# Transposing the second norm's rows by DMA instead of on TensorE, in a fused WKV mixer and mixture-of-experts kernel

## What is computed

```
x = x + wkv(w, u, layernorm(x), ctx)                     # 2048 rows of 512
y = layernorm(x)
probs = softmax(y @ gate_w.T);  top 2 of 8 experts per row
moe = sum over the 2 chosen e of prob_e * (silu(y @ gate_e.T) * (y @ up_e.T)) @ down_e.T     # width 256
shared = sigmoid(y @ g.T) * (silu(y @ sg.T) * (y @ su.T)) @ sd.T                             # width 1024
x = x + moe + shared
```

## Time and profile before

| | |
|---|---|
| median of 3 runs | 564.96 us (562.85 to 565.99) |
| profiled execution | 566.06 us, its span 564.3 us |
| PE busy (TensorE) | 486.2 us, 86% |
| DVE busy (VectorE) | 421.3 us, 75% |
| POOL busy (GpSimd) | 345.4 us, 61% |
| ACT busy (ScalarE) | 275.9 us, 49% |
| DMA | q0 (GpSimd's) 21.3%, q1 (SyncE's) 18.5% of the 16 engines' span, the latter for 37.59 MB |
| chain that ended last | PE 52%, POOL 17%, issue 10%, DVE 9%, DMA 7%, ACT 3% |

### The profile page before, as it was taken

One profiled execution on the slowest core, in us unless ns is written; L12 is line 12 of the kernel. 1 busy time (PEld: TensorE's weight loads), 2 busy tenths in 40 slices (PEclk: granted clock), 3 DMA queues, 4 the chain that ended last, 5 costly groups with the idle time before them and its releaser, 6 DMA issues.

```text
span 564.3 us, 10142 instructions
## 1 busy us (share of the span) xinstructions
PE 486.2 (86%) x2671; PEld 258.5 (46%) x2671; DVE 421.3 (75%) x954; ACT 275.9 (49%) x534; POOL 345.4 (61%) x422
## 2 busy tenths in 40 slices
PE   1116789899999999999999979999999999999970
PEld 1113345345455555454555435445545555555530
DVE  5678987899989899999898867566656656666650
ACT  4848837575573864765837333433333333333310
POOL 5767956857948669588486364334375565555332
PEclk9999989999999999999999999999999999999995
DMA  7970105105213223151101320315576776677453
GB/s 283 415 271 19 38 19 187 57 21 188 76 46 143 77 82 143 38 188 62 52 20 39 105 88 15 113 45 102 101 122 117 141 119 116 110 131 123 69 73 38
DMA packets 25929, 59.14 MB, mean 105 GB/s; under 512 B 6314, under 2 KB 6314, under 8 KB 24338
## 3 DMA queue, kind: packets, MB, share of 16 engines
q0 software_dynamic: 9824, 20.90, 21.3%
q1 hardware_dynamic: 16050, 37.59, 18.5%
HBM read 37.83 MB, written 20.65 MB: 104 GB/s over the span
## 4 chain that ended last, share of the span: by engine, by line
PE 52%; POOL 17%; issue 10%; DVE 9%; DMA 7%; ACT 3%; SPq 1%; POOLq 0%; DVEq 0%; ACTq 0%
PE GU L884 28%; PE DN L899 14%; DMA out<-wall,idsa 5%; POOL wall L445 4%; PE XT L829 3%; PE HT L829 3%; POOL yb L429 2%; POOL nrm L411 2%; POOL nrm L413 2%; DVE wall L1071 2%; POOL wall L424 2%; POOL wall L421 2%; DVE wall L1078 1%; PE YT L829 1%; SPq L366 1%
## 5 line engine op out<-in xcount | busy, mean ns | idle before, releaser
L884 PE MATMUL GU<-wall,xt 128*128 128x512 f16 x768 | 187.0, 384 | 2.1 <-DVE wall L1173 2.0
L899 PE MATMUL DN<-wall,hx 128*128 128x512 f16 (+1 forms) x618 | 150.8, 380 | 7.2 <-DVE hx L1200 4.5
L884 PEld LDWEIGHTS GU<-wall,xt 128*128 128x128 f16 x768 | 74.8, 99 | 70.4 <-issue 3.7
L584 POOL DMA_INDIRECT out<-wall,idsa x39 | 62.0, 1590 | 73.1 <-SPq L370 35.1
L659 ACT ACTIVATE hx<-HT 128x256 f16<-128x256 f32 x103 | 39.0, 379 | 127.4 <-PE HT L829 110.6
L899 PEld LDWEIGHTS DN<-wall,hx 128*128 128x128 f16 x618 | 60.4, 98 | 81.9 <-issue 6.0
L1200 DVE TENSOR_TENSOR hx<-HT,hx 128x256 f16<-128x256 f32 x103 | 43.1, 418 | 64.3 <-ACT hx L659 59.7
L654 ACT ACTIVATE th<-GU,scl 128x256 f32<-128x256 f32 x103 | 48.5, 471 | 80.0 <-PE GU L884 76.1
L884 PE MATMUL GU<-wall,kb 128*128 x240 | 61.4, 379 | 0.2 <-DVE kb L1374 0.2
L884 PE MATMUL GU<-wall,xnb 128*128 x228 | 58.5, 379 | 0.6 <-DVE xnb L1374 0.6
L574 POOL DMA_INDIRECT xb<-xn_rows,idsi x39 | 40.2, 1030 | 30.5 <-DMA out<-xb 16.3
(11 more groups left out here) (163 smaller groups left out, 747.3 us busy)
## 6 DMA issues: line engine op xcount, KB each, us to landing
wall<-wgu SPq DMA_DIRECT2D x12, 1024.0 KB, 9.7
wall<-wd SPq DMA_DIRECT2D x12, 512.0 KB, 10.3
out<-xb SPq DMA_DIRECT2D x20, 256.0 KB
xb<-x SPq DMA_DIRECT2D x16, 256.0 KB, 2.7
cb<-ctx_t SPq DMA_DIRECT2D x16, 256.0 KB
xn_rows<-xnb SPq DMA_DIRECT2D x16, 256.0 KB
xb<-xn_rows,idsi POOLq DMA_INDIRECT x39
out<-wall,idsa POOLq DMA_INDIRECT x39
```

The source lines that it names most:

```text
L584: pool.indirect_dma_start(out, bass.IndirectOffsetOnAxis(ap=idsa[:, j:j + 1], axis=0), ye[j % RESULTS], None, compute_op=ALU.add).then_inc ...
L884: ins = nc.tensor.matmul(GU[par][:], lhs(xp, c), gate_up(base, wp, c), start=m == 0, stop=m == 3 * HC - 1)
L899: ins = nc.tensor.matmul(DN[:], hx[par][:, hp * IE + c * P:hp * IE + (c + 1) * P], down(base, wp, c), start=start and m == 0, stop=stop an ...
```

## The change

The second norm's rows are split into halves where they are rows, and the pair is transposed by a DMA on SyncE's queue.

- **Mix.** `norm` puts the factor XS = 1024 into the scale. ScalarE writes xnb in float32 and then, in a second instruction over the same row, the high half as float16 into a new buffer xr. VectorE makes the low half as xnb minus the high half, from SBUF. SyncE then issues `turn_xn`, one DMA transpose of 128 x 1024 float16 (256 KB) from xr into xt, eight blocks of 128 x 128. The four transposes of XT, `xn_t_` and `act_hi` are gone, and the bank XT too. `store_xn` stores the pair xr (as many bytes as before) and waits for the low half.
- **Order in the mix.** On VectorE `act_lo` stands before the last reciprocal and before `hidden(n + 2)` instead of after it. On SyncE the store of the sum goes ahead of the transpose, the store of xn and the load of x behind it. The router and the shared units wait for the transpose (`x_turned`).
- **End of the mix.** SyncE's queue after the last turn is: `turn_xn(15)`, then the load of expert 7, then the stores.
- **Routed phase.** The gather brings rows that are already split. `gathered_t`, `gathered_hi` and `gathered_lo` are gone; one DMA transpose per slot (`turn_gathered`) writes one of now four buffers xe. The first four are issued before the last `store_sum`. The transpose of slot j+3 stands in SyncE's queue at the head of step j, that is behind the permission of add j-1 and ahead of that of add j. It waits for its gather and for the slot four before to be used up. A gather into a buffer waits for the transpose that read it.
- Small tables move into the context buffer cb to make room, and less_r shrinks to four columns that are broadcast.

The core of the diff (declarations, semaphore lists and small moves of tables left out):

```diff
+        xr = sb("xr", [P, 2 * H], F16)
...
-        xe = [kb[:, :].bitcast(F16), xnb[:, :].bitcast(F16)]
+        xe = [kb[:, :].bitcast(F16), xnb[:, :].bitcast(F16), xt[:, 2 * H:4 * H], yb[:, :].bitcast(F16)]
+        XE = len(xe)
...
+            def turn_xn(t):
+                sp.wait_ge(x_lo, t + 1)
+                wait_from(sp, x_turned, t * 16)
+                wait_from(sp, gu, (t - NX + 1) * SU)
+                wait_from(sp, logits, t - NX + 1)
+                sp.dma_start(span(xt, (t % NX) * (2 * H), 2 * H).rearrange("p (c t) -> p c t", t=P), xr[:],
+                             transpose=True).then_inc(x_turned, 16)
+            def turn_gathered(j):
+                r = j % GATHERS
+                sp.wait_ge(gather[r], 16 * (j // GATHERS + 1))
+                if j >= XE:
+                    sp.wait_ge(gu, N_EXP + j - XE + 1)
+                    sp.wait_ge(g_turned[j % XE], 16 * (j // XE))
+                sp.dma_start(xe[j % XE].rearrange("p (c t) -> p c t", t=P), xg[r][:, 0:H].bitcast(F16),
+                             transpose=True).then_inc(g_turned[j % XE], 16)
             def store_xn(t):
-                sp.wait_ge(xn_rdy, t + 1)
-                sp.dma_start(rows(xn_dram, t)[:, 0:H], xnb[:]).then_inc(xn_st, 16)
+                sp.wait_ge(x_lo, t + 1)
+                wait_from(sp, xn_st, t * 16)
+                sp.dma_start(rows(xn_dram, t)[:, 0:H], xr[:, :].bitcast(F32)).then_inc(xn_st, 16)
...
-                if i == 1:
-                    load_expert(1)
...
-                if i > 0:
+                if i > 0 and j is None:
+                    turn_xn(i - 1)
                     store_xn(i - 1)
+                    load_expert(1)
                 if j is not None and j > 0:
                     store_sum(j - 1)
+                if j is not None:
+                    turn_xn(i - 1)
+                    store_xn(i - 1)
...
             sp.wait_ge(y_rdy, B)
+            turn_xn(B - 1)
             load_expert(E - 1)
...
+            for j in range(XE):
+                turn_gathered(j)
             store_sum(B - 1)
             sp.wait_ge(waits_rdy, WAIT_STEPS)
             for j in range(1, NSLOT):
+                if j + XE - 1 < NSLOT:
+                    turn_gathered(j + XE - 1)
...
             def second_norm(t):
                 act.wait_ge(norm2, (t + 1) * NORM_STEPS)
-                wait_from(act, xn_t, t)
-                wait_from(act, xn_st, 16 * t)
+                wait_from(act, x_lo, t)
                 nc.scalar.activation(xnb[:], xrow(t), ACT.Identity, bias=nrm[:, 1, 3:4],
                                      scale=nrm[:, 1, 2:3]).then_inc(xn_rdy, 1)
+                wait_from(act, xn_st, 16 * t)
+                wait_from(act, x_turned, 16 * t)
+                nc.scalar.activation(xr[:, 0:H], xrow(t), ACT.Identity, bias=nrm[:, 1, 3:4],
+                                     scale=nrm[:, 1, 2:3]).then_inc(x_hi, 1)
...
-                pe.wait_ge(g_lo, j + 1)
+                pe.wait_ge(g_turned[j % XE], 16 * (j // XE + 1))
...
             def act_lo(t):
+                dve.wait_ge(xn_rdy, t + 1)
                 dve.wait_ge(x_hi, t + 1)
-                STT(xt_row(t, 1), XT[:], XS, xt_row(t, 0), ALU.mult, ALU.subtract).then_inc(x_lo, 1)
+                TT(xr[:, H:2 * H], xnb[:], xr[:, 0:H], ALU.subtract).then_inc(x_lo, 1)
...
                 hidden_lo(n + 1, 1)
+                act_lo(i - 1)
                 reciprocals(i, 3, 1)
                 hidden(n + 2, 0, SHARED)
-                act_lo(i - 1)
```

More of the change, by code:

```diff
@@ L175, in build @@
         r_cmp, r_eid, r_row, r_one, r_of = taken(NSLOT * E), taken(NSLOT), taken(E), taken(E), taken(2)
+        eidi, idsi, idsa, wsl, pad_of = (taken(NSLOT) for _ in range(5))
+        eidi, idsi, idsa, before_i = (a.bitcast(I32) for a in (eidi, idsi, idsa, taken(RESULTS * NSLOT)))
         ids_back, ids_float = by_time[0:NSLOT, 0:P * LW].bitcast(I32), yb[0:NSLOT, 0:P]
@@ L410, in norm @@
                 wait_from(pool, used, t)
-                nc.gpsimd.tensor_scalar(nrm[:, k, 0:1], mv[:, k, 1:2], EPS, None, ALU.add).then_inc(steps, 1)
+                nc.gpsimd.tensor_scalar(nrm[:, k, 0:1], mv[:, k, 1:2], EPS, XS ** -2 if k else 1.0, ALU.add,
+                                        ALU.mult).then_inc(steps, 1)
                 pool.wait_ge(steps, t * NORM_STEPS + 1)
@@ L506, in _ @@
             second_product(1)
-            norm(0, 1, agg2, norm2, xn_rdy)
+            norm(0, 1, agg2, norm2, x_hi)
             scales(1, SHARED)
@@ L527, in turn @@
                     shared_d_lo(0)
-                norm(i - 1, 1, agg2, norm2, xn_rdy)
+                norm(i - 1, 1, agg2, norm2, x_hi)
                 if i == LAG:
@@ L549, in _ @@
             expert_lo(E - 2, 2)
-            norm(B - 1, 1, agg2, norm2, xn_rdy)
+            norm(B - 1, 1, agg2, norm2, x_hi)
             scatter(B - 4)
@@ L721, in _ @@
             d_square(3)
-            act_hi(0)
             shared_gu_hi(0)
@@ L757, in turn @@
                 unit_tanh(n + 2, 0, SHARED)
-                act_hi(i - 1)
                 if i + 2 < B:
@@ L784, in _ @@
             router_out(B - 2)
-            act_hi(B - 1)
             unit_hi(n, 0)
@@ L820, in _ @@
             for j in range(NSLOT):
-                expert_unit(j, j % 2, ahead=j < NSLOT - 1)
+                expert_unit(j, j % 2)
             unit_hi(N_EXP + NSLOT - 1, 0)
@@ L840, in y_back @@
                 transposes(YT, yb, HC, y_t)
[L842 to L845 removed]
             def router(t, sums_before=None):
[L848 removed]
+                pe.wait_ge(x_turned, 16 * (t + 1))
                 if isinstance(t, int) and t == 0:
@@ L968, in _ @@
             turns(turn, LAG)
-            def gathered_t(j, r):
-                pe.wait_ge(gather[r], 16 * (j // GATHERS + 1) if isinstance(j, int)
-                           else ((j - r) // GATHERS) * 16 + 16)
-                wait_from(pe, g_lo, j)
-                transposes(XT, xg[r], HC, g_t)
             def listed_before(t):
@@ L1380, in _ @@
             hidden(n, 0, SHARED)
+            act_lo(B - 1)
             small_steps(t=B - 2)
[L1382 removed]
             choices(B - 2)
@@ L1448, in _ @@
             for j in range(NSLOT):
-                expert_unit(j, ahead=j < NSLOT - 1)
+                expert_unit(j)
                 if 0 < j < 3:
```

57 lines of the change are left out of this document (14 added, 43 removed).

## The result

The change makes the kernel slower: 617.85 us (616.01 to 619.27, four runs) against 564.99 us (562.85 to 565.99, four runs), a ratio of 1.094 with a 95% interval from 1.089 to 1.098. The forecast was 573 and its range ended at 590. The sign was right, the size was missed by 45 us.

The account below looks back on a forecast made before the run. TensorE was taken to bound the routed phase and the mix's odd turns. Routed phase 2.4, end of mix 3.0 and turns 3.0 gave +8.4 on 566.06, 574.5; the median, 1.1 lower, was rounded to 573 us, range 555 to 590.

Parts of the forecast that it names:

- the pace of slots 9 to 38: Routed phase: 29 slots at 4.10 us, 118.9, plus 10.2 of stalls; slot 38 starts 2.4 us later.
- the turns of the mix: Mix: extra ScalarE pass and earlier low half delay HT; worst case 6 us over 6.5 pairs, half taken, +3.0.
- T: Time from SyncE's issue of a 256 KB transpose to its landing: 3.4 us, near bounds 2.7 and 4.0.
- rival 4: Transposes turn blocks one after another, T 9.7 us: about 656 us in total; chance 0.03.
- Slots of 4.10: Routed phase: without the XT transposes, 0.44 us of TensorE's time, a slot falls from 4.54 to 4.10 us.
- the start of the routed phase: Adds 5.70 us apart hold transposes 5 to 9; slot 9 starts at 412.3 us, before the change 405.85.
- T - 1.7: Routed phase: average stall at each of six changes of expert, 10.2 us in all at T 3.4.
- rival 3: Routed phase: SyncE or the DMA engines set the pace; at 2.5 us per issue slots take 5.05, total 591; chance 0.12.
- The end of the mix: Last router starts at 336.9 us instead of 333.88, after second norm pass, low half and transpose: +3.0.
- The freed VectorE and ScalarE time: Routed phase: time saved on halves of gathered rows is worth nothing, since neither engine bounds a slot.

Follow-up runs that it names:

- e15: Kernel before with 35 plain 256 KB copies added to SyncE's queue in the routed phase, in place of e8's unused transposes: 575.25 us.
- e4: Kernel after without transposes from slot 4 on, TensorE multiplying what the first four left (output not the reference's): 578.36 us.
- e17: Kernel after with e9's early subtraction, a fifth buffer of turned rows and constants for SyncE's permission reads: beat its expected 586 to 591 us by 7 us.
- e13: Kernel after with a fifth buffer for turned rows, so routed transposes are issued a slot sooner: 618.31 us.
- e3: Kernel after with transposes of 128 KB instead of 256 KB from slot 4 on (low halves stale): 613.33 us.
- e9: Kernel after with the low-half subtraction act_lo(i - 1) moved ahead of reciprocals(i, 1, 2) on VectorE in the mix: 616.22 us.
- e7: Kernel after without ScalarE's float32 norm pass in the mix, low half made from unnormalised rows (output not the reference's): 613.11 us.
- e8: Kernel before with 35 transposes of 256 KB, whose result nobody reads, added to SyncE's queue in the routed phase: 593.55 us against 565.51.
- e11: Kernel before with e8's 35 unused transposes, all writing one buffer, and constants for the permissions' register reads: 578.22 us.
- e10: Kernel after with the four register reads of a permission put ahead of the same step's transpose on SyncE: 643.17 us.
- e1: Kernel after with the routed transposes from slot 4 on issued by ScalarE behind a tanh instead of by SyncE: 639.68 us.

## Why the prediction was wrong

The forecast of +8.4 became +52.9 at the median. Two steps of the sum failed: the pace of slots 9 to 38, and the turns of the mix.

**T** was right: 3.1 and 3.6 us against 3.4. The Trainium skill ("Advanced Engine Details and Errata", X-Bar Transpose) has transposing DMAs as fast as regular ones. By landing that nearly holds here (2.8 for a load of x of that size); by the issue it does not (1.23 against 0.47 us in e15), and the issue was what counted. The Trainium skill's 1309 ns for a 128 x 128 block ("VectorE: DVE Perf Modes", The three transpose paths) do not add up block by block here: eight blocks landed in 3.1 us, so rival 4 is out.

**Slots of 4.10** were right (e4; e17 at its end), and so in the main was **the start of the routed phase**: transposes 5 to 9 held by the adds, which come 5.5 to 6.3 us apart for the 5.70 taken, slot 9 48.7 us after slot 0 by forecast (412.3 - 363.63), 50.3 measured. e13 shows the cause: with one buffer more slots 0 to 9 take 44.7, so 5.6 of the 8.1 us go. Another 1.2 are slot 0 itself (6.03 us for 4.83), at a granted clock of 0.68 behind its wait.

**Slots 9 to 38** are the first step that failed. I let TensorE set 4.10 and charged T - 1.7 at six changes of expert, 129.1 in all; it was 154.4. The arithmetic that would have told stood in rival 3: "if issuing a transpose holds it for over 1.55 us it sets the pace". The issue is 1.23, below that point, and by that sum a step of SyncE was 3.78 us and fitted into 4.10. The mistake is in the other addend: the 2.55 us of reads was a price from a queue with nothing else in it. Behind a transpose the same reads take 3.4 to 3.7 us (496.73 to 500.08 in the chain of the kernel after), which makes 4.6 to 5.1. Rival 3 was the right mechanism with a threshold from undisturbed rows; it got 0.12. Its price for the DMA engines was too low as well: by the growth of q1's share over 55 transposes, one takes some 1.7 us of all 16 engines, not 0.7. That was not the pace, as e3 and e17 show.

The chain of the kernel after shows that step, from issue to the grant:

```profile
495.46 1.24 SPq L301
...
496.73 0.63 SPq L397
...
497.73 0.27 SPq L397
...
498.37 0.73 SPq L397
...
499.45 0.26 SPq L397
...
500.87 4.89 DMA out<-wall,cb
505.80 0.04 issue
```

Nor does the step stand alone. It ends in the permission, the add lands 4.9 us later and the next transposes are queued behind that landing. That fits constants helping by 22 us in the kernel after and by 3 in the one before.

**The turns of the mix** are the second. The worst case was +0.9 us for a pair of turns, of which I took half; it is +1.9 (four pairs by the loads of context: 133.78 to 284.95, 37.8 each, before; 137.10 to 295.78, 39.7 each, after). The low half was priced at 0.68 us, from the PSUM form of the earlier trace rows. It takes 1.33 beside GpSimd's products, a wait that the sum put at nothing. At 0.65 for both turns of a pair that would cover the gap, but only part of it is shown: e9 takes 0.5 away per turn and gets back 4.7 of the 10.8 us by which the last load of context is late. I expected ScalarE's second pass to weigh as much; e7 shows that it hardly does (1 us). The rest of the 10.8 is open.

Of the 15.4 us up to the last xnb 4.6 come behind that load, and the rows account for them. VectorE's product of the probabilities takes 2.0 longer in the last turn (shown at e9), and TensorE stands behind it:

```profile
330.34 0.44 PE L847 MATMUL HT<-ident,hb 128*128 128x128 f32 x2 [2.67 <-DVE hb L1198]
330.62 2.42 PE L897 MATMUL GU<-wall,xt 128*128 128x512 f16 x6
```

Before, HT waited 0.71 there. From 330.60 to 334.90 the granted clock is 0.60, and two groups of six matmuls take 2.42 and 2.15 for 1.46 each, which is 1.2 net of XT. The last 1.4 is about the wait for hb of the turn before (1.25).

**The end of the mix** was right (+2.5 for +3.0: TensorE waited 3.10 us for the last transpose). **Slot 0** then waited 2.62 us more for its rows, where the sum had nothing: its transpose, issued at 376.31 beside gathers and with more transposes behind it, landed some 8 us later.

**The freed VectorE and ScalarE time** in the routed phase gave nothing that shows, as foretold.

## What to carry to other kernels

Price a step moved to a DMA queue by what it holds the issuing engine for, and add that to everything else this engine has to do per step; leave a margin, because here the register reads behind it got slower too. Where the engine also grants permissions, try the change first with unused transfers in the kernel before (e8): one run, and it would have told 28 of the 50 us. Give these transfers as many buffers as the real ones, or they wait for each other, as in e11. An instruction moved from PSUM to SBUF operands on VectorE has a new price: here 0.69 or 1.33 us, by where it stood against GpSimd's products.

## What the runs showed that I had not expected

- A transposing DMA is issued in 1.23 us for 256 KB and 1.19 to 1.22 us for 128 KB; a plain copy of 256 KB in 0.47. The four in a row ahead of slot 0 took 1.23, 1.99, 3.42 and 1.59 us.
- Register reads on SyncE take 0.38 us at the median behind transposes of the same queue, against 0.27 in the kernel before, when they come first (e10), behind plain copies (e15), and with the transposes on ScalarE's queue (e1). Single ones take up to 0.9 to 1.2 us in each of these runs.
- A product of VectorE on two SBUF operands took 0.27 us when it began just ahead of GpSimd's, 2.23 when it began just behind.
- The DMA share of e17 is 1.05, with slots near 4.10: a share of 0.90 in the kernel after did not mean that the DMA engines set the pace.
- Behind some waits of TensorE the granted clock is lower: 0.60 from 330.60 to 334.90, behind a wait of 2.67 us, and 0.68 from 384.70 to 387.10, behind one of 2.62; over 380 to 450 us it is 0.90, where it was 1.00 before. The six matmuls at 384.70 took 2.37 us where six take 1.46, so part of them ran at the lower of the two levels (1.2 for 2.4 GHz).
